# Deformable-convolution kernel, strip stage: a third PSUM bank for the wide products, and half of the weighted rows added on VectorE before the transposes

## The reference

```python
# block 0
offset = conv3x3(gn(x)); cols = bilinear samples of gn(x) at 9 taps + offset
x = x + relu(bn(einsum(cols, w_dcn)))
# block 1 (modulated, twice)
out = gelu(bn(deform(gn(x), offset1, sigmoid(m1), w_dcn1)))
out = bn(deform(out, offset2, sigmoid(m2), w_dcn2))
x = x + gelu(out + gn(x))
```

## Time and profile before

| | |
|---|---|
| median of 3 runs | 8342.6 us (8338.94 to 8348.57) |
| the profiled execution | 8339.3 us, its span 8337.5 us |
| PE busy over the span | 6098.2 us (73%) |
| DVE | 4698.9 us (56%) |
| ACT | 2008.5 us (24%) |
| POOL | 5533.2 us (66%) |
| TensorE clock, mean share of full | 0.817 |

### The profile page before, as it was taken

How to read it: one execution, slowest core, us unless ns; L and a number is a source line. 1 busy time by engine, 2 the same in 40 slices (tenths; PEclk the granted TensorE clock), 3 DMA queues, 4 the chain that set the end, 5 groups by cost and what they waited for, 6 DMA issues and landing times. The chain is left out here.

```text
span 8337.5 us, 110679 instructions
## 1 busy us (share of the span) xinstructions
PE 6098.2 (73%) x38788; PEld 4405.1 (53%) x38788; DVE 4698.9 (56%) x10889; ACT 2008.5 (24%) x3025; POOL 5533.2 (66%) x5485
## 2 busy tenths in 40 slices
PE   7996777875777765777863323359998998998998
PEld 5774555553555554555642211136666666666665
DVE  5665666664666664666653222235565656556666
ACT  1111112121111121111121111113333343333443
POOL 0004777777777777777777777776667667666776
PEclk9997888886888876888875555569898998889999
DMA  4222333332333332333322221222233322322332
GB/s 123 71 71 77 92 90 91 92 90 76 88 88 90 88 88 78 92 88 86 92 82 64 57 52 51 52 64 73 74 76 81 77 74 71 85 77 66 86 77 73
DMA packets 376814, 658.97 MB, mean 79 GB/s; under 512 B 121336, under 2 KB 279352, under 8 KB 368696
## 3 DMA queue, kind: packets, MB, share of 16 engines
q0 software_dynamic: 175104, 358.96, 17.0%
q1 hardware_dynamic: 201272, 294.06, 11.4%
HBM read 610.22 MB, written 42.42 MB: 78 GB/s over the span
## 5 line engine op out<-in xcount | busy, mean ns | idle before, releaser
L708 POOL DMA_INDIRECT G<-table,IDX x5472 | 5519.1, 1009 | 2759.6 <-issue 2306.4
L1124 ACT ACTIVATE SAMP<-RED 96x384 f32<-96x384 f32 x1216 | 591.4, 486 | 5147.9 <-PE RED L877 2219.9
L1649 DVE TENSOR_TENSOR ARENA<-ARENA 128x288 f32<-128x288 f32 x3744 | 1457.4, 452 | 543.5 <-PE RED L892 525.3
L892 PE MATMUL RED<-IDENT,ARENA 128*96 128x128 f32 x11232 | 1514.4, 295 | 302.7 <-DVE ARENA L1649 302.7
L892 PEld LDWEIGHTS RED<-IDENT,ARENA 128*96 128x96 f32 x11232 | 1341.5, 137 | 460.8 <-issue 402.1
L1527 DVE TENSOR_TENSOR G<-G,W 128x1152 f32<-128x1152 f32 x540 | 734.5, 1360 | 1362.0 <-DMA G<-table,IDX 1356.5
L950 PE MATMUL BTP<-PAD,ARENA 80*128 x3456 | 1259.8, 478 | 245.1 <-DVE PAD L1520 125.3
L877 PE MATMUL RED<-IDENT,SUM 128*96 128x128 f32 x1248 | 291.4, 357 | 1472.4 <-DVE SUM L1541 1464.0
L877 PEld LDWEIGHTS RED<-IDENT,SUM 128*96 128x96 f32 x1248 | 148.8, 154 | 1590.7 <-DVE SUM L1541 1169.7
L802 PE MATMUL OFFC<-PAD,ARENA 128*54 128x256 f32 (+3 forms) x3726 | 965.1, 418 | 27.4 <-ACT PAD L1051 15.3
L950 PEld LDWEIGHTS BTP<-PAD,ARENA 80*128 80x128 f32 x3456 | 595.1, 199 | 667.4 <-issue 581.6
(11 more groups left out here) (169 smaller groups left out, 4413.0 us busy)
## 6 DMA issues: line engine op xcount, KB each, us to landing
ARENA<-wtab SPq DMA_DIRECT2D x208, 800.0 KB
G<-table,IDX POOLq DMA_INDIRECT x5472
ARENA<-xo SPq DMA_DIRECT2D x96, 720.0 KB
table<-TB SPq DMA_DIRECT2D x64, 384.0 KB, 2.8
X<-x SPq DMA_DIRECT2D x2, 3200.0 KB, 22.3
out<-X SPq DMA_DIRECT2D x20, 320.0 KB
wtab<-TB SPq DMA_DIRECT2D x16, 384.0 KB, 2.9
PAD<-x SPq DMA_DIRECT2D x4, 800.0 KB, 6.7
```

The lines of the kernel that those rows point to most:

```text
L708: pool.indirect_dma_start(G[:, b, k, :], None, tables[seg.table], bass.IndirectOffsetOnAxis(ap=IDX[:, q, b * TAPS + k:b * TAPS + k + 1], a ...
L892: last = nc.tensor.matmul(RED[b % 2][0:TPG * C, gr * 128:(gr + 1) * 128], PROD[gr][:, sft, :], IDENT[:, :], start=(sft == 0), stop=(sft == ...
L1124: nc.scalar.activation(SAMP[:, x], RED[x][0:TPG * C, 0:GROUPS * 128].rearrange("p (g n) -> p g n", g=GROUPS), ACT.Copy).then_inc(z.samp_re ...
L1649: last = nc.vector.tensor_tensor(out=PROD[gr][:, :, j * C:(j + 1) * C].rearrange("p (dy dx) c -> p dy dx c", dy=3), in0=win[:, gr:gr + 3, ...
```

## The change

Three banks take the taps in turn, the third one being OUT[1]; in the main C2 stage the two outputs of a round then share the bank OUT[0], 256 columns each, and the waits for `out_read` and `projected` are widened to both. A new DVE instruction, `fold`, follows each group's products: it adds rows 5 to 9 of `PRODS[gr]` onto rows 0 to 4 (128x480 float32, both inputs in SBUF), and `reduce` waits for it and issues five transposes in place of ten.

```diff
@@ -34,6 +34,7 @@
 WENT = ENTRIES + EDGE
 NTB = 3
 GBUF = 3
+TAPB = 3
 PREP = 13
 TENTS, TENTS_AT = 4, 8
 REACH = 1.0
@@ -41,6 +42,7 @@
 CHUNKS = 4
 STRIPS, SROWS, SCOLS, SFIRST = 12, 4, 64, 16
 WY = 10
+WF = WY // 2
 TAPW = WY * C
 MARGIN, LOWEST, HIGHEST = 3.5, -14, 6
 
@@ -164,6 +166,8 @@
         OFFT = ps("OFFT", [128, 512])
         RED = [ps(f"RED{i}", [128, 512]) for i in range(2)]
         OUT = [ps(f"OUT{i}", [128, 512]) for i in range(2)]
+
+        TAP = BTP + [OUT[1]]
 
         x_first = [sem(f"x_first{c}") for c in range(CHUNKS)]
         x_loaded = sem("x_loaded")
@@ -199,6 +203,7 @@
         tx_ready = sem("tx_ready")
         taps = sem("taps")
         weighted = sem("weighted")
+        folded = sem("folded")
         xt_psum = sem("xt_psum")
         xt_evac = [sem("xt_evac_s"), sem("xt_evac_v")]
         w_zeroed = sem("w_zeroed")
@@ -294,8 +299,11 @@
         def past(n, least):
             return not (isinstance(n, int) and n < least)
 
+        def out_slot(seg, po):
+            return OUT[0][:, po * 256:(po + 1) * 256] if seg.z is main and seg.s == C2 else OUT[po][:, 0:256]
+
         def out_tile(seg, po):
-            return OUT[po][rows(seg.p), 0:256]
+            return out_slot(seg, po)[rows(seg.p), :]
 
         SETUP = 15
         NORM = 21
@@ -851,10 +859,10 @@
                     z = seg.z
                     pe.wait_ge(z.samp_ready, v + 3)
                     if b == 0:
-                        pe.wait_ge(z.out_read, u + 1)
+                        pe.wait_ge(z.out_read, u + 2 if z is main and seg.s == C2 else u + 1)
                     at = seg.p % 2 * R2 + b % 2 * C
                     for gr in range(GROUPS):
-                        last = nc.tensor.matmul(OUT[po][at:at + C, b // 2 * 128:(b // 2 + 1) * 128], WDCN[:, seg.s, gr, :],
+                        last = nc.tensor.matmul(out_slot(seg, po)[at:at + C, b // 2 * 128:(b // 2 + 1) * 128], WDCN[:, seg.s, gr, :],
                                                 SAMP[:, x, gr, :], start=(gr == 0), stop=(gr == GROUPS - 1))
                     last.then_inc(z.projected, 1)
 
@@ -905,6 +913,7 @@
                     pass
 
                 def calibrate(n):
+                    pe.wait_ge(main.out_read, U_C2 + 2)
                     for e in tb_evac:
                         pe.wait_ge(e, ITS * (KB["t", PAIRS] + 1))
                     pe.wait_ge(strip_setup, 6)
@@ -944,21 +953,21 @@
                     for j in range(TPG):
                         k = TPG * gr + j
                         c = 36 * si + 9 * b + k
-                        if c > 1:
-                            pe.wait_ge(weighted, c - 1)
+                        if c >= TAPB:
+                            pe.wait_ge(weighted, c + 1 - TAPB)
                         row = strip_row(s, k0) + 2 * tt + k // 3 - 1 + LOWEST
-                        nc.tensor.matmul(BTP[c % 2][:, 0:TAPW], TXB[tt][:, im, k, :],
+                        nc.tensor.matmul(TAP[c % TAPB][:, 0:TAPW], TXB[tt][:, im, k, :],
                                          XT[:, bass.ds(bases[k] + (im * H + row) * C, TAPW)],
                                          start=True, stop=True).then_inc(taps, 1)
 
                 def reduce(now, b, gr):
                     if gr == 0:
                         pe.wait_ge(main.samp_ready, unit(now.u, b, 1) + 1)
-                    pe.wait_ge(weighted, 36 * (now.s.first + now.k) + 9 * b + 3 * gr + 3)
-                    for w in range(WY):
+                    pe.wait_ge(folded, 12 * (now.s.first + now.k) + 3 * b + gr + 1)
+                    for w in range(WF):
                         last = nc.tensor.matmul(RED[1][0:TPG * C, gr * 128:(gr + 1) * 128],
                                                 PRODS[gr][:, w, :], IDENT[:, :],
-                                                start=(w == 0), stop=(w == WY - 1), is_transpose=True)
+                                                start=(w == 0), stop=(w == WF - 1), is_transpose=True)
                     last.then_inc(prod_used, 1)
 
                 def turn_sums(now, b):
@@ -978,7 +987,7 @@
                     for gr in range(GROUPS):
                         for kind, im in enumerate((b % 2, strip_unit(b) % 2)):
                             at = now.g.p % 2 * R2 + im * C
-                            last = nc.tensor.matmul(OUT[(now.u + kind) % 2][at:at + C, b // 2 * 128:(b // 2 + 1) * 128],
+                            last = nc.tensor.matmul(out_slot(now.g, (now.u + kind) % 2)[at:at + C, b // 2 * 128:(b // 2 + 1) * 128],
                                                     WDCN[:, C2, gr, :], SAMP[:, kind, gr, :], start=(gr == 0), stop=(gr == GROUPS - 1))
                             if gr == GROUPS - 1:
                                 last.then_inc(main.projected, 1)
@@ -1518,8 +1527,13 @@
                         c = 36 * si + 9 * b + k
                         dve.wait_ge(taps, c + 1)
                         nc.vector.tensor_tensor(
-                            out=PRODS[gr][:, :, j * C:(j + 1) * C], in0=BTP[c % 2][:, 0:TAPW].rearrange("p (w c) -> p w c", w=WY),
+                            out=PRODS[gr][:, :, j * C:(j + 1) * C], in0=TAP[c % TAPB][:, 0:TAPW].rearrange("p (w c) -> p w c", w=WY),
                             in1=TY[now.k % 2][:, strip_unit(b) * TAPS + k, :].unsqueeze(2).to_broadcast([128, WY, C]), op=ALU.mult).then_inc(weighted, 1)
+
+                def fold(now, b, gr):
+                    dve.wait_ge(weighted, 36 * (now.s.first + now.k) + 9 * b + 3 * gr + 3)
+                    nc.vector.tensor_tensor(out=PRODS[gr][:, 0:WF, :], in0=PRODS[gr][:, 0:WF, :], in1=PRODS[gr][:, WF:, :],
+                                            op=ALU.add).then_inc(folded, 1)
 
                 def scale(z, m, q, b):
                     dve.wait_ge(z.gathered[b], 16 * TAPS * (m + 1))
@@ -1549,7 +1563,7 @@
                                                    in1=T1[ps_, po], op0=ALU.mult, op1=ALU.add).then_inc(z.pre_gelu, 1)
 
                 def before_gelu(now, kind):
-                    on.add_residual(now.s if kind else now.g, now.u + kind, (now.u + kind) % 2, unit(now.u, UNITS - 1, kind))
+                    on.add_residual(now.s if kind else now.g, now.u + kind, (now.u + kind) % 2, unit(now.u, UNITS - 1, 1))
 
                 def after_gelu(now, kind):
                     on.finish(now.s if kind else now.g, now.k, now.u + kind, (now.u + kind) % 2)
@@ -1558,12 +1572,14 @@
                     m, q = now.g.first + now.k, slot(now.g, now.k)
                     for b in range(UNITS):
                         on.weight_rows(now, b, 0)
+                        on.fold(now, b, 0)
                         on.scale(main, m, q, b)
                         if before and b == 1:
                             on.before_gelu(before, 1)
                         if before and b == 2:
                             on.after_gelu(before, 0)
                         on.weight_rows(now, b, 1)
+                        on.fold(now, b, 1)
                         on.halve(main, m, b)
                         if sprep and b == 1:
                             on.prepare_strip(0, *sprep)
@@ -1572,6 +1588,7 @@
                         if gprep and b == 3:
                             on.place(*gprep)
                         on.weight_rows(now, b, 2)
+                        on.fold(now, b, 2)
                         on.sum_up(main, m, b)
                         if before and b == 0:
                             on.before_gelu(before, 0)
```

## The result

The changed kernel took 8045.2 us (median of 5 runs, 8038.3 to 8062.8) against 8348.6 us for the kernel before on the same chip: a ratio of 0.9637, 95% interval 0.962 to 0.9655, some 300 us less. Forecast were 8137 us and a gain of 205 us, with a range of 8040 to 8260. The sign was right and the range held the time, 5 us above its low end. The same kernel on another chip later took 8024.0 us, beside 8338.8 for the kernel before; that lies under the range.

The account below looks back on a forecast made before the run. PE sets the pace of C2 now, POOL after the change. Gathers 1883, gaps 524 + 35, folds 63, tail 17 and waits 13 and 32 make 2567 us instead of 2772.5, 205 less: 8137 us, range 8040 to 8260.

Parts of the forecast that it names:

- POOL becomes the bound: C2 stage: POOL needs 49.0 us per round, 636 us per pair, above the 618 of PE and DVE.
- The waits, 13 and 32 us: POOL's idle time in C2: 13 us in the first unit, 20 in the first pair, 12 for uneven feeding.
- rounds with builds at 51 us: PE and DVE in a C2 round with a build: 43 us plus 2.5 for the build and 5 to 6.6.
- the half clock: PE in C2 rounds with builds: 10 to 14 us at half clock, adding 5 to 6.6 us.
- The folds' delay of the gathers, 63 us: POOL in C2: gathers starting during a fold wait for it, 0.11 us on average for each of 576 folds.
- the rival of 8042 us: C2 gathers: folds do not slow them and waits are few, so 8042 us without 63 and 32; chance 0.12.
- The change on PE: C2 stage: half the transposes go and waits for taps shrink; with DVE's work, a plain round takes 43 us.
- 6.5 us of transposes: PE in C2: half of the transposes go, saving 6.5 us per round.
- 4.2 + 2 us of waits: PE in C2: the third bank removes third-tap waits, 4.2 us per round, and the 2.00 us standstill during `place`.
- The clock: Rival: PE, less busy in C2, is granted 0.81, so rounds take 51.2 us, 54 with a build: 8240 us; chance 0.20.
- No gain, by the weight loads' share: Rival: TensorE's weight loads at 64% lie under POOL's 68%, so removing transposes buys little; within 0.2%, chance 0.04.
- 0.53 x 576: Upper end of the folds' delay of C2 gathers, if each fold catches a gather's start: given as 302 us.

Follow-up runs that it names:

- g2: The changed kernel with six of the nine gathers of each C2 unit, the other three taps of G keeping old data: 7846.4 us.
- g3: The changed kernel with three banks but no fold, ten transposes, and six of nine gathers in each C2 unit: 7863.7 us.

## Why the prediction was right, and what was off

- **POOL becomes the bound: right.** The gathers, their gaps and the tail gave a floor of 2459 us for the stage, which no saving on PE could go under. The profile has 1884 + 560 + 18 + 17 = 2479 us; this execution reached the stage some 16 us later, with 13 more gathers left behind 5565 us.
- **The waits, 13 and 32 us: too many.** Measured, 18 us in all. I had rounds with builds at 51 us, slower than the gathers; they take 47.2 without the gathers (g2). That is 4.8 above the plain round's 42.4; less the 2.5 us that I took for the build itself, some 2.3 us are left for the half clock, where I had charged 5 to 6.6. This is an estimate, and it puts the mis-sized term there. Why the half clock costs so little is open. DVE alone is not the bound in these rounds: in the eight shown above (g2, 379.07 us) it waits for PE's taps for 52 us. With the bank alone (g3) they take 379.90 us at a granted 0.97 in place of 0.88, with more work on PE. No run took the clock apart.
- **The folds' delay of the gathers, 63 us: the mechanism right, the sum wrong.** A gather that starts in a fold does wait. One of the changed kernel, issued in a fold:

```profile
7054.24 0.66 DVE L1535 TENSOR_TENSOR PAD<-PAD 128x480 f32<-128x480 f32 x1
7054.36 1.36 POOL L716 DMA_INDIRECT G<-table,IDX  x1 [0.30 <-issue]
```

  1.36 us, by the rule (rest of the fold, less 0.13) 0.41 longer than 0.95. Some 155 gathers were held up so, 42 to 44 us in sum, and at least eight in ten of them ended 0.817 to 0.822 us behind the fold's end. But I added this to an unchanged rest, and the rest changed: delays in `scale` fell from 76 to 42 us and in `halve` from 57 to 26 (in `sum_up` up from 8 to 16), presumably since DVE now waits for gathers and its phase is no longer random against them. The mean gather went from 1025 to 1019 ns, not to 1060. So the rival of 8042 us had the time right and its reason wrong: that it came within 3 us is luck, and so is part of the range, whose low end it gave. It also had a sentence of the Trainium skill (SBUF — State Buffer, Who interferes with whom) behind it, marked there as inferred, that a tensor_tensor does not stall such DMAs; the rows above and the weights in PSUM speak against that sentence. These two terms, 63 and 32, are the 95 us between 8137 and 8042.
- **The change on PE: the sum of its parts hid that one is worth nothing.** I counted 6.5 us of transposes and 4.2 + 2 us of waits as savings of one chain, found 43 us for the round (42.4 measured), and never walked the parts apart. My own figures had the answer: 41.8 us of PE work with all transposes, 40.5 of DVE work with the fold. For the bank alone I expected 45 us from this walk; it was 42.3, since PE waits for no product there. The gain of 300 us is the bank's.
- **The clock: milder than the rival.** 0.86 against the 0.81 feared. The half clock grew from 3.1 to 11.2 us per round of the last pair, in the shadow of the gathers. With one transpose per group in place of five it was 25.7, and POOL waited for the chain for 47 us more. No row shows the factor 1.75 by which that rival slowed the chain.
- **No gain, by the weight loads' share: wrong here.** They were at 64%, and yet PE was on the path. With the bank alone PE never waits and they are at 79% (366.8 of 465.4 us), so a share well under 100% is no slack. The Trainium skill (Perfetto Trace Analysis, Identifying the Most-Contended Engine) would have TensorE judged by this share together with its share of the peak rate; in this kernel the waits judge it better.
- **A slip in a bound.** 0.53 x 576 is 305 us, not 302. The forecast does not use it.

## What to carry to other kernels

Walk each part of a change by itself against the next bounds: a buffer that lets the slow engine run ahead and a move of work to its neighbour may each look like the gain, and here the first was all of it and the second a loss of 0.8% by itself. Before relieving an engine, add up the busy time, gaps and waits of every queue that runs beside it; the time it can give back is the smallest sum of their waits. Where a GpSimd queue of indirect DMAs is the bound, count two-SBUF-input VectorE instructions as its cost, and put a small operand into PSUM if a bank is free.

## What was not expected of the hardware

- A `scale` with one operand in PSUM delays gathers by about 1 us in sum (some 180 that started in one), with both in SBUF by 42 us (some 200). Two SBUF inputs where one is broadcast, such as `scale`'s weights, count as two.
- Less work came with a lower clock and no time: with 2304 transposes fewer the last pair ran at a granted 0.73 against 0.88, and its rounds went from 47.2 to 48.2 us. The gathers bound the kernel, so there was nothing to gain; the loss goes with POOL's longer waits.
- The bank alone, with more work on PE, had the higher clock: 1.00 in the last pair of g3, against 0.96 in g2.
- That the folds' and the scales' delays change places by phase is read from sorting the gathers; no run set the phase on purpose. Why the stages ahead of C2 took some 16 us more in the changed kernel's first profile is open; their code is the same, and in its later profile they did not (1836 gathers behind 5565 us, where the first had 1850 and the kernel before 1837).
